# Attention and a mixture of experts on one core: expert tiles scaled on VectorE and added into the output by accumulating DMAs

## What is computed

```python
x = x + xattn(layernorm(x), ctx, ...)      # 16 heads of 16, context of 154 rows, output projection
x = x + ffn(layernorm(x), ...)             # 8 experts, 2 of them per token, and a shared one
...
_, sel = jax.lax.top_k(scores + expert_bias, TOP_K)
top_scores = jnp.take_along_axis(scores, sel, axis=1)
top_scores = top_scores / (top_scores.sum(-1, keepdims=True) + EPS)
shared = jax.nn.silu(x @ Wg_s) * (x @ Wu_s) @ Wd_s
h = jax.nn.silu(jnp.einsum('nd,edf->enf', xr, Wg)) * jnp.einsum('nd,edf->enf', xr, Wu)
out_all = jnp.einsum('enf,efd->end', h, Wd)
routed = (routed * w[:, None])
out = shared.at[tok].add(routed)
```

## Time and profile before

| | |
|---|---|
| Median of 3 runs | 698.19 us (696.99 to 698.49) |
| The profiled execution's own time | 697.73 us |
| Its span | 695.9 us |
| TensorE, VectorE, ScalarE, GpSimd busy | 76%, 55%, 30%, 27% of the span |
| DMA | 74.00 MB, mean 106 GB/s |
| Mean granted clock of TensorE | 0.87 of full speed |

### The profile page before, as it was taken

One profiled execution on the slowest core, in us unless ns is written; L12 is line 12 of the kernel. 1 busy time (PEld: TensorE's weight loads), 2 busy tenths in 40 slices (PEclk: granted clock), 3 DMA queues, 4 the chain that ended last, 5 costly groups with the idle time before them and its releaser, 6 DMA issues.

```text
span 695.9 us, 10007 instructions
## 1 busy us (share of the span) xinstructions
PE 525.8 (76%) x2952; PEld 327.2 (47%) x2953; DVE 385.3 (55%) x913; ACT 211.1 (30%) x431; POOL 188.9 (27%) x202
## 2 busy tenths in 40 slices
PE   5558799999999896446401389999999999999500
PEld 4443255555554334323200256666766766767300
DVE  4974788888888544682000044444544544445286
ACT  0446577577577540200000011122222222222000
POOL 4354211211210000007777400003334333333300
PEclk9868999999999897559655589999999999999855
DMA  8707322422421301104223111313233232232198
GB/s 266 250 1 242 76 77 77 139 91 77 140 74 62 115 24 27 60 15 137 105 100 122 69 45 46 90 34 118 76 106 106 80 114 82 100 122 64 48 366 310
DMA packets 53277, 74.00 MB, mean 106 GB/s; under 512 B 6143, under 2 KB 42815, under 8 KB 52800
## 3 DMA queue, kind: packets, MB, share of 16 engines
q1 hardware_dynamic: 41216, 48.38, 22.1%
q0 software_dynamic: 7808, 21.05, 8.7%
q10 hardware_dynamic: 4224, 4.19, 1.7%
HBM read 38.86 MB, written 35.79 MB: 107 GB/s over the span
## 4 chain that ended last, share of the span: by engine, by line
PE 55%; DVE 24%; another core or an unknown queue 12%; DMA 4%; issue 2%; ACT 2%; SPq 1%; POOL 1%; POOLq 0%; DVEq 0%; ACTq 0%
PE bankS L844 19%; PE bankS L860 12%; DVE rec L1030 8%; PE bankV L754 6%; PE bankR L629 4%; PE bankV L758 2%; DMA experts<-y_rows 2%; DVE X L1243 2%; DVE OTT L1032 2%; PE bankQ L851 2%; PE bankR L851 2%; PE bankS L629 1%; PE bankS L741 1%; DVE xstat L933 1%
## 5 line engine op out<-in xcount | busy, mean ns | idle before, releaser
L462 POOL DMA_INDIRECT y_rows<-VR,attn x72 | 70.0, 972 | 192.8 <-DVE VR L1215 170.6
L609 ACT ACTIVATE scores_in<-bankS 128x192 f32<-128x192 f32 x104 | 34.2, 330 | 265.2 <-PE bankS L844 168.2
L844 PE MATMUL bankS<-experts,scores_in 128*128 x288 | 103.5, 492 | 1.8 <-ACT scores_in L600 0.3
L1197 DVE TENSOR_TENSOR scores_in<-scores_in,bankS 128x192 f32<-128x192 f32 x104 | 36.7, 354 | 122.6 <-ACT scores_in L609 95.4
L457 POOL DMA_INDIRECT sorted_rows<-XR,attn x64 | 62.4, 975 | 112.2 <-DVE XR L1178 93.0
L543 ACT ACTIVATE attn<-bankS,bias 128x512 f32<-128x512 f32 x128 | 79.8, 682 | 17.2 <-PE bankS L729 17.1
L860 PE MATMUL bankS<-experts,scores_in 96*128 x288 | 74.1, 380 | 0.0
L754 PE MATMUL bankV<-attn,VS 128*32 128x512 f32 x256 | 64.2, 624 | 7.6 <-DVE OTT L1032 7.6
L844 PEld LDWEIGHTS bankS<-experts,scores_in 128*128 128x128 f32 x288 | 51.7, 190 | 33.3 <-issue 9.0
L756 PE MATMUL bankD<-attn,ON 128*32 128x512 f32 x256 | 64.2, 624 | 0.0
L860 PE MATMUL bankS<-wds_sb,scores_in 96*128 96x256 f32 x128 | 37.4, 426 | 27.1 <-issue 27.1
(11 more groups left out here) (202 smaller groups left out, 829.8 us busy)
## 6 DMA issues: line engine op xcount, KB each, us to landing
sorted_rows<-XR SPq DMA_DIRECT2D x12, 774.0 KB, 5.1
VS<-sorted_rows SPq DMA_DIRECT2D x36, 258.0 KB
experts<-y_rows SPq DMA_DIRECT2D x16, 512.0 KB, 9.2
x_cols<-X2T SPq DMA_DIRECT2D x16, 256.0 KB, 2.1
scores_in<-x_cols SPq DMA_DIRECT2D x16, 256.0 KB
out<-X ACTq DMA_DIRECT2D x8, 512.0 KB, 7.1
x_in<-in_xT POOLq DMA_DIRECT2D x15, 256.0 KB, 5.3
experts<-in_wgu SPq DMA_DIRECT2D x2, 1536.0 KB, 8.9
```

Of the source, the lines that this page charges most:

```text
L462: pool.indirect_dma_start(y_rows, bass.IndirectOffsetOnAxis(ap=dest[:, i:i + 1], axis=0), y_out[:, i % 4], None, bounds_check=2 * B * N - ...
L844: last = pe.matmul(gate_bank(k)[:, 0:2 * F], x_col[:, k, c * P:(c + 1) * P], rhs, start=(c == 0), stop=(c == KC - 1))
L1197: dve.tensor_tensor(h_in[:, k % 2], act_g[:, k], gate_bank(k)[:, F:2 * F], ALU.mult).then_inc(f_h[kind], 1)
```

## The change

`y_rows`, its loads, the 64 weighted additions and the 8 stores at the end are gone. In their place:

- **Output written early.** While the shared expert runs, GpSimd stores each finished quad of `X1` (residual plus shared result) to `out`, 8 DMAs of 512 KB, once the scatter is issued.
- **Accumulating DMAs.** `result` multiplies the bank by the slot's weight (a column of `w_slot`) in place of the copy, and GpSimd's indirect DMA adds the tile to the rows of `out`. As both results of a token go to one row, tiles of different experts may not be in flight together. Within one expert every token stands once.
- **The wait.** For each slot, GpSimd reads four numbers from the table `gate` into registers and waits until the four semaphores `y_st` have reached them. The numbers say how many tiles of all earlier experts belong to each semaphore, so they rise only where the expert changes. They start at `BASE` = 32, the count of the early stores.
- **Rows.** A sorted row has four extra numbers in place of two: token, expert key and both weights. `places` picks the weight for the slot's expert and copies the token number to `dest`, for 10 small operations per quad in place of 4.
- **Filler rows** now carry a number in 512 spare rows behind `out`, with weight zero, and are written too. SyncE first stores 512 KB of `X1` there. The fill of `sorted_rows` is 18 DMAs of 4 slots in place of 12 of 6.
- **SyncE's loads** for the shared expert are written out, with no loop, register waits or `aside`.

```diff
-ROW = D + 2
+ROW = D + 4
-NOWHERE = 1 << 15
+NOWHERE = B * N
-FILLS = 12
-CT = 4
-CS = 4
+FILLS = 18
+SPARE = 4 * P
+QUADS = TILES // 4
+BASE = 16 * QUADS // 4
...
             for m in range(LATE):
                 store(m)
-                if m < FILLS:
-                    few = SLOTS // FILLS
-                    sp.dma_start(sorted_rows[few * m:few * (m + 1)].rearrange("s p r -> p s r"),
-                                 empty.unsqueeze(1).to_broadcast([P, few, ROW])).then_inc(filled, 16)
+                for i in range(2 * m, min(2 * m + 2, FILLS)):
+                    sp.dma_start(sorted_rows[4 * i:4 * i + 4].rearrange("s p r -> p s r"), empty).then_inc(filled, 16)
...
+            sp.dma_start(out[B * N:].rearrange("(a p) d -> p a d", p=P), X1[:, 0:4, :]).then_inc(spare_set, 16)
+
+            for a in range(QUADS):
                 for h in range(2):
-                    if not isinstance(a, int) or a >= 1:
+                    if a >= 1:
                         sp.wait_ge(f_gu["s"], 4 * a + (2 * h - 2))
-                    aside(sp)
-                    sp.dma_start(x_col[:, 2 * h:2 * h + 2], x2_cols[ds(2 * a + h, 1), :, :].rearrange("o p (t c) -> p (o t) c", t=2)) \
-                        .then_inc(f_ld["s"][h], 16)
-            quads(sp, TILES, load_shared)
+                    sp.dma_start(x_col[:, 2 * h:2 * h + 2], x2_cols[2 * a + h].rearrange("p (t c) -> p t c", t=2)).then_inc(f_ld["s"][h], 16)
 
             for i in range(4):
...
             for i in range(4):
-                sp.wait_ge(y_st[i], 4 * SLOTS)
-            y_t = y_rows.rearrange("(k t p) d -> p k t d", k=2, p=P)
-            for c in range(TILES // CT):
-                if c >= CS:
-                    sp.wait_ge(c_sum, c - CS + 1)
-                for k in range(2):
-                    sp.dma_start(ya[:, c % CS, k * CT:(k + 1) * CT], y_t[:, k, c * CT:(c + 1) * CT]).then_inc(c_ld[c % CS], 16)
-            sp.wait_ge(s_out, 16 * (TILES // CT))
...
+            out_t = out[0:B * N].rearrange("(t p) d -> p t d", p=P)
+            for a in range(QUADS):
+                pool.wait_ge(f_yd["s"], 4 * a + 4)
+                pool.dma_start(out_t[:, 4 * a:4 * a + 4], X1[:, 4 * a:4 * a + 4]).then_inc(y_st[a % 4], 16)
+            pool.wait_ge(spare_set, 16)
             for i in range(SLOTS):
+                for k in range(4):
+                    landed = pool.value_load(gate[0:1, k, i:i + 1], min_val=BASE, max_val=BASE + 4 * SLOTS)
+                    pool.wait_ge(y_st[k], landed)
+                    aside(pool)
                 pool.wait_ge(f_yd["e"], i + 1)
-                pool.indirect_dma_start(y_rows, bass.IndirectOffsetOnAxis(ap=dest[:, i:i + 1], axis=0),
-                                        y_out[:, i % 4], None, bounds_check=2 * B * N - 1, oob_is_err=False).then_inc(y_st[i % 4], 16)
+                pool.indirect_dma_start(out, bass.IndirectOffsetOnAxis(ap=dest[:, i:i + 1], axis=0), y_out[:, i % 4], None,
+                                        bounds_check=B * N + SPARE - 1, oob_is_err=True, compute_op=ALU.add).then_inc(y_st[i % 4], 16)
...
-            for c in range(TILES // CT):
-                act.wait_ge(c_sum, c + 1)
-                act.dma_start(out.rearrange("(t p) d -> p t d", p=P)[:, c * CT:(c + 1) * CT], X1[:, c * CT:(c + 1) * CT]).then_inc(s_out, 16)
...
+            padded = small[:, 13, 0:E]
+            link(dve.tensor_copy(padded, a_))
...
+            link(dve.tensor_tensor(wide, wide, padded.unsqueeze(1).to_broadcast([P, SLOTS, E]), ALU.mult))
+            link(dve.tensor_reduce(before, wide, AX, ALU.add))
+            link(dve.tensor_scalar(before, before, 1.0 / P, None, ALU.mult))
+            for k in range(4):
+                last = dve.tensor_scalar(gate[:, k], before, float(3 - k), None, ALU.add)
+            link(last)
+            link(dve.tensor_scalar(gate, gate, 2, 4, ALU.arith_shift_right, ALU.logical_shift_left))
+            link(dve.tensor_scalar(gate, gate, BASE, None, ALU.add))
+
+            dve.tensor_copy(XR[:, :, D], tokens)
+            for k in range(2):
+                last = dve.tensor_copy(XR[:, :, D + 2 + k], wts[:, k])
+            link(last)
             dve.tensor_scalar(XR[:, :, D + 1], small[:, 2], -1.0, float(E), ALU.mult, ALU.add).then_inc(routed, 1)
...
-                    dve.tensor_tensor(dest_f[:, h], x_row[:, 2 * h:2 * h + 2, D + 1], etf[:, ds(4 * a + 2 * h, 2)], ALU.not_equal).then_inc(e_chain, 1)
-                    dve.wait_ge(e_chain, 2 * a + (h + 1))
+                    of_row = lambda c: x_row[:, 2 * h:2 * h + 2, D + c]
+                    dve.tensor_copy(dest[:, ds(4 * a + 2 * h, 2)], of_row(0))
+                    dve.tensor_tensor(sel[:, 0], of_row(1), etf[:, ds(4 * a + 2 * h, 2)], ALU.is_equal).then_inc(e_chain, 1)
+                    dve.wait_ge(e_chain, 4 * a + (2 * h + 1))
+                    dve.tensor_tensor(sel[:, 1], sel[:, 0], of_row(2), ALU.mult)
+                    dve.scalar_tensor_tensor(out=sel[:, 2], in0=sel[:, 0], scalar=-1.0, in1=of_row(3), op0=ALU.add, op1=ALU.mult).then_inc(e_chain, 1)
+                    dve.wait_ge(e_chain, 4 * a + (2 * h + 2))
                     aside(dve)
-                    dve.scalar_tensor_tensor(out=dest[:, ds(4 * a + 2 * h, 2)], in0=dest_f[:, h], scalar=float(B * N),
-                                             in1=x_row[:, 2 * h:2 * h + 2, D], op0=ALU.mult, op1=ALU.add).then_inc(e_dst, 1)
+                    dve.tensor_tensor(w_slot[:, ds(4 * a + 2 * h, 2)], sel[:, 1], sel[:, 2], ALU.subtract).then_inc(e_dst, 1)
...
-                                dve.wait_ge(y_st[k], 16 * a)
+                                dve.wait_ge(y_st[k], BASE + 16 * a)
+                            dve.wait_ge(e_dst, 2 * a + (k // 2 + 1))
                             aside(dve)
-                            dve.tensor_copy(y_out[:, k], down_bank(k)).then_inc(f_yd["e"], 1)
+                            w_k = w_slot[:, ds(4 * a + k, 1)]
+                            dve.tensor_tensor(y_out[:, k], down_bank(k), w_k.to_broadcast([P, D]), ALU.mult).then_inc(f_yd["e"], 1)
...
-            for c in range(TILES // CT):
-                dve.wait_ge(c_ld[c % CS], 32 * (c // CS + 1))
-                for k in range(2):
-                    for t in range(CT):
-                        tile = c * CT + t
-                        last = dve.scalar_tensor_tensor(out=X1[:, tile, :], in0=ya[:, c % CS, k * CT + t], scalar=wts[:, k, tile:tile + 1],
-                                                        in1=X1[:, tile, :], op0=ALU.mult, op1=ALU.add)
-                    if k == 0:
-                        last.then_inc(c_half, 1)
-                        dve.wait_ge(c_half, c + 1)
-                last.then_inc(c_sum, 1)
...
-    a["fill_c"] = np.zeros((P, ROW), np.float32)
-    a["fill_c"][:, D] = NOWHERE
+    a["fill_c"] = np.zeros((P, 4, ROW), np.float32)
+    a["fill_c"][:, :, D] = NOWHERE + np.arange(SPARE).reshape(4, P).T```

On GpSimd, behind the 64 scatters, stood 72 indirect DMAs in one row (names: `y_rows` and `sorted_rows` in HBM, VR the buffer `y_out`, attn the memory that holds index tables):

```order
L457 DMA sorted_rows<-XR,attn 9216x258 x64
L462 DMA y_rows<-VR,attn 8192x256 x72
L79 UNCONDITIONAL_BRANCH
```

More of the change, by code:

```diff
@@ L76, in build @@
 def build(nc, x, xT, ctxT, wq, wkv, wp, bp, ln_g, ln_b, centre, ident, ident16, own, wr, wgu, wd, wgu_s, wd_s, e_bias, tri_c, rev_c, tok_c, tst_c, fill_c,
-          x2_cols, sorted_rows, y_rows, out):
+          x2_cols, sorted_rows, out):
     ctx = ExitStack()
@@ L161, in build @@
         early_x = [x_in[:, 0], x_in[:, 1], OTT[:, 0].rearrange("p k t -> p (k t)")[:, 0:KC * TT * P].rearrange("p (k t) -> p k t", k=KC)]
-        empty = XR[:, TILES - 1, :]
+        empty = XR[:, TILES - 4:, :]
         wgu_sb, wd_sb = views(experts[:, :], (KC, E, 2 * F), (FC, E, D))
-        ya, = views(experts[:, :], (CS, 2 * CT, D))
         (tri, ones, ebias, rev, tokens, tstart, ex, sc, sbias, cand, oh1, oh2, cum_a, cum_b, slot, small, etf, wts, pos_f, etile, pos,
-         wide, dest_f, dest) = views(attn[:, :], (P,), (P,), (E,), (E,), (TILES,), (SLOTS,), *[(TILES, E)] * 9, (16, TILES), (SLOTS,), (2, TILES),
-                                     (2, TILES), (SLOTS,), (2, TILES), (SLOTS, E), (2, 2), (SLOTS,))
+         wide, sel, w_slot, dest, before, gate) = views(attn[:, :], (P,), (P,), (E,), (E,), (TILES,), (SLOTS,), *[(TILES, E)] * 9, (16, TILES), (SLOTS,), (2, TILES),
+                                     (2, TILES), (SLOTS,), (2, TILES), (SLOTS, E), (3, 2), (SLOTS,), (SLOTS,), (SLOTS,), (4, SLOTS))
         etile = etile.bitcast(I32)
@@ L171, in build @@
         dest = dest.bitcast(I32)
+        gate = gate.bitcast(I32)
         x_col, act_g, h_in, h_col = views(scores_in[:, :], (4, D), (4, F), (2, F), (4, D))
@@ L244, in build @@
         x2t_st = [sem("x2t_st0"), sem("x2t_st1")]
-        s_out = sem("s_out")
         filled = sem("filled")
         fill_in = sem("fill_in")
```

(19 more changed lines are left out.)

2 lines of the change are left out of this document (removed).

## The result

The changed kernel takes **717.04 us** (median of 4 runs, 716.23 to 718.99); the kernel before, run beside it, 697.59 (696.94 to 698.49). The ratio is 1.0277, 95% interval 1.0252 to 1.0302: slower, where 670.4 and faster were forecast. 717.0 lies outside the range of 662 to 706.

What follows compares the result with a forecast made beforehand. Three stages with three limits, the expert stage bound by TensorE. -41.04 + 7.2 + 0.1 + 0.5 + 3.9 + 2 = -27.3 us on 697.73 gives 670.4 us (forecast 662 to 678, range with rivals 662 to 706).

Steps and rivals of the forecast that it cites:

- The gates: Per expert slot, GpSimd's four register loads take 1.42 us beside the DMA's 1.29, under 2.68; counted at nothing.
- the first: Expert stage: register loads push GpSimd over 2.68 us a slot, making the kernel slower; 703 us or more; chance 0.17.
- The second: Expert stage: GpSimd just over the bound, 2.75 to 3.05 us a slot; about 682 us; chance 0.12.
- The third: Expert stage: accumulations land after over 9.5 us, so VectorE and TensorE stall at result buffers; 713 us; chance 0.04.
- the fourth: Shared expert's standstill during the scatter lifts, as SyncE's loads lose register waits; down to 612 us; chance 0.05.
- The real waits: At slots 31, 32, 64 and 65 GpSimd stands 1 to 7 us; buffers leave 9.5; counted at nothing.
- The accumulation: Accumulating DMA of expert tiles: lands after 2.4 to 9.2 us; 0.75 us of DMA time per tile, hidden.
- Taking away the end: The stretch after the last expert tile's issue, with only the combination in it, goes: -41.04 us.
- the DRAIN: GpSimd closing its stream at the kernel's end, no longer covered by the combination: +7.2 us.
- Routing: New small operations ahead of the scatter lie on the path: +3.9 us (3 to 5).
- `places`: Expert stage: up to 1.4 us more per quad, delaying each of 17 quads by 0.1; +2 us (0 to 8).

Runs made afterwards that it cites:

- e3_loads_bounds: Changed kernel with four bounds-checked loads per slot, no waits on them, each slot adding into spare rows of its own; 625.77 us against 638.05.
- one-load kernel: Changed kernel with one flag load per slot instead of four, wait values computed in registers; 668.13 us beside 697.19, later 616.04 beside 638.05.
- e1_plain_store: Changed kernel with its gates kept, but the indirect DMA stores instead of adding; 714.96 us, ratio 1.0244.
- e3_changed: The changed kernel itself run again, unaltered, on another chip; 667.15 us beside 638.05 for the kernel before, ratio 1.0451.
- e2_before_unrolled: The kernel before with the shared expert's six middle quads written out instead of looped; 637.05 us, ratio 0.9996.
- third set: The last of three sets of runs, each on its own chip; here the kernel before took 638.05 us.

## Why the prediction was wrong

**The failed step** is "The gates": "Four are 4 x (302 + 18 + 34) = 1.42 us", and from it "Then a slot takes the larger of 1.42 and 1.29 us", with the gates put at nothing. The overlap was read rightly: the sequencer does run beside the engine. What was mis-sized is the sequencer's own row of work, 4 x 0.65 + 0.50 = 3.11 us a slot and not 1.42. Three things were missing:

- The register operation behind each load, 0.15 us. The view of the kernel before from which the earlier trace rows are taken lists it on TensorE too, and I passed it over. Four times 0.15 is 0.6 us.

```profile
L822 PEldq FUSED_REGOPS  x120: 46/151/168, 459.6 to 646.1; - x120
```

- The gaps between such instructions. I added up durations. The pitch of one load with its check (from its start to the next one's) is 0.55 us where the durations say 0.45, and a register wait with `aside` is 0.10 where I had put 0.034.
- The 0.50 us in which the sequencer hands over an indirect DMA. Before, it hid behind the engine's 0.97 us, and in the working it had no place. It holds the sequencer, so it adds to the gates.

The earlier trace rows were read rightly and proved too little. That the sequencer ran 15 us ahead in the scatter means that it needs less than the engine when a slot is a MOVE and a dispatch. It says nothing of a slot with twelve more rows of work.

The Trainium skill (DMA: Bandwidth & Descriptors, "Latency and other measured facts") has about 600 ns as a tensor load's floor. The load itself takes 288 ns here, less than half. But what a program pays per bounds-checked load is 0.55 us, and with the wait 0.65. I set the page's figure aside because of one duration, when it was near to the price of the whole gate. As an estimate by that figure, a slot would have been 4 x 0.6 + 0.50 = 2.9 us, over TensorE's; my text said that it still hides, for want of the 0.50.

**The rivals.** What happened is the first, GpSimd as the bound, with its place and its threshold (3.06 us by that text; measured 3.11 in the even steps and 3.355 in the mean). By its own rule, 71 x (3.355 - 2.68) = 48 us more than 670.4 is 718, and 717.0 was measured. I gave it 0.17 and took it to need 0.6 us or more per load. It needed only what every gate costs. The second had the same place and ended just short, at 3.05 us. The third (landings over 9.5 us) fell with landings of 5.3 us at the longest (e3_loads_bounds), and the fourth fell too: the earlier trace rows's 24.69 us is 24.71.

**The real waits** were counted at nothing. The cover named there was the 9.5 us that the buffers leave. It holds only if GpSimd can catch up afterwards, and with its spare time gone they cost 9.5 us (by chance the same number). In the one-load kernel GpSimd has time to spare again and they cost nothing, as the seven steps of 1.84 to 1.91 us show.

**The accumulation** was bounded by 2.4 and 9.2 us for its landing, measured 3.8 in the median. Its DMA time was taken as twice a store's, 0.75 us a tile; it is three times, 1.1 us, and hides as was said. That it holds the engine 1.54 us instead of 0.97 was nowhere in the working. It decided nothing: e1_plain_store has the same distance.

**What held.** Taking away the end: -41.04 + 7.4 = -33.6 us, by the DRAIN, not the landing, as put (+7.2; the DRAIN ends 7.1 us after the last DMA's start). Routing: +3.6 against +3.9, by the scatter's first DMA (315.1 against 311.5). The new operations are 3.2 of it: from the first product over 128x576 to that DMA are 3.49 us before and 6.73 after. The rest is drift from ahead of them; that product starts anywhere from 306.55 to 310.37 us in runs of the changed kernel's routing. The steps: with the gates out of the way, the mean one is 0.02 us longer than before, 1.5 us in all against the 2 that I put down to `places`, which no run tested by itself. The one-load kernel's span, 668.0, is 27.9 us below the 695.9 of before, and splits into -41.04 + 7.3 + 4.3 + 1.5. The forecast had -41.04, then 7.8 for the end, 3.9 for routing and 2, so it is in effect that of the one-load kernel. That 4.3 is so near to 3.9 is luck: about 2 are its shorter routing and 2 are drift. That e3_changed ran in 667 us is no support for it, since the kernel before stood at 638 beside it.

## What to carry to other kernels

A sequencer is an engine with a budget of its own: when a change gives it work per tile, add up the pitch of every instruction it issues, from start to start, with the dispatch of its DMAs, and compare the sum with the bound's pace per tile. Durations of single rows are too small for that; a stretch in which the same sequence repeats gives the price. If values from memory steer a queue, load one and compute the rest in registers: here that turned a loss of 2.8% into a gain of 4.3%, and on the chip of the third set a loss of 4.5% into a gain of 3.3%.

## What the runs showed of the hardware

- GpSimd's sequencer is held 0.50 us by each indirect DMA, and 0.55 us by a bounds-checked load, of which the load proper is 0.29.
- An accumulating indirect DMA of 128 rows of 1 KB holds the engine 1.54 us against 0.97 for a store, lands after 3.8 us in the median (3.5 to 5.3 over the runs) against 2.4, and takes three times the packets and DMA engine time.
- With one real wait at each slot, a slot takes 4.85 us.
- The DRAIN of GpSimd ends 7.1 to 7.2 us after the last accumulating DMA starts, 3.3 to 3.4 us after SyncE sees it landed. Behind plain stores (e1_plain_store) it ends 7.8 us after the last start, so it doesn't follow the landing.
- The 60 us in which the shared expert stands still beside the scatter belong to the chip or its conditions; the runs don't tell these apart. In e2_before_unrolled the same 64 DMAs take the same time (311.50 to 392.18) and TensorE does 75 of 86 us of work beside them, with 24.69 in the earlier trace rows. What holds the semaphores up there stays open.
